# First self attention of a decoder: ScalarE instead of GpSimd makes the high halves of the next pair's weights

## The reference

```python
q, k, v = split_heads(x @ Wq), split_heads(x @ Wk), split_heads(x @ Wv)   # 16 heads of 128
q = _apply_rope(q, cos, sin)
k = _apply_rope(k, cos, sin)
scores = jnp.einsum('bhqd,bhkd->bhqk', q, k) * scale
scores = jnp.where(causal[None, None], NEG_INF, scores)
attn = jax.nn.softmax(scores, axis=-1)
ctx = jnp.einsum('bhqk,bhkd->bhqd', attn, v)
...
x = _layernorm(x + _L0_attn_ref(x, L0_attn_Wq, L0_attn_Wk, L0_attn_Wv, L0_attn_Wo), axis=-1)
```

## Time and profile before

| what | value |
|---|---|
| median of three runs | 2584.72 us (2582.74 to 2585.06) |
| the profiled execution | 2586.08 us, its span 2584.2 us |
| TensorE busy | 2410.7 us, 93% |
| VectorE busy | 1848.7 us, 72% |
| ScalarE busy | 1578.1 us, 61% |
| GpSimd busy | 882.4 us, 34% |
| mean granted clock of TensorE | 0.974 of full speed |

### The profile page before, as it was taken

One profiled execution on the slowest core, in us unless ns is written; L12 is line 12 of the kernel. 1 busy time (PEld: TensorE's weight loads), 2 busy tenths in 40 slices (PEclk: granted clock), 3 DMA queues, 4 the chain that ended last, 5 costly groups with the idle time before them and its releaser, 6 DMA issues. The chain is left out here.

```text
span 2584.2 us, 57959 instructions
## 1 busy us (share of the span) xinstructions
PE 2410.7 (93%) x21584; PEld 1560.9 (60%) x21584; DVE 1848.7 (72%) x3371; ACT 1578.1 (61%) x2718; POOL 882.4 (34%) x800
## 2 busy tenths in 40 slices
PE   7999998989999999999998999999999999999874
PEld 4555555556766677665465666765566666665332
DVE  5777777757777777875665666666678888883597
ACT  5777776258888888884235565652477777772242
POOL 5666666634433444354142122235100011013111
PEclk9999999999999999999998999999999999999987
DMA  3433334426666766676422434353388777787200
GB/s 94 89 75 89 77 88 106 128 46 117 118 123 122 117 115 118 121 128 149 158 91 52 96 86 93 94 112 111 58 146 145 145 146 147 143 150 154 59 1 33
DMA packets 769429, 273.84 MB, mean 106 GB/s; under 512 B 737904, under 2 KB 740720, under 8 KB 767600
## 3 DMA queue, kind: packets, MB, share of 16 engines
q1 hardware_dynamic: 767504, 265.82, 49.8%
q0 software_dynamic: 1760, 5.77, 0.8%
HBM read 84.55 MB, written 6.44 MB: 35 GB/s over the span
## 5 line engine op out<-in xcount | busy, mean ns | idle before, releaser
L909 ACT ACTIVATE phl<-p,ri 128x1024 bf16<-128x1024 f32 (+4 forms) x512 | 437.4, 854 | 382.2 <-DVE ri L1228 355.6
L1238 DVE SCALAR_TENSOR_TENSOR phl<-p,ri,phl 128x1024 bf16<-128x1024 f32 (+4 forms) x512 | 513.6, 1003 | 143.9 <-issue 122.7
L922 ACT ACTIVATE p<-p,nb 128x1024 f32<-128x1024 f32 (+4 forms) x512 | 435.8, 851 | 52.6 <-DVE nb L1221 38.6
L1305 PE MATMUL ps<-wo_lo,v_hi 128*128 128x128 bf16 x2496 | 441.3, 220 | 0.0
L1304 PE MATMUL ps<-wo_hi,v_hi 128*128 128x128 bf16 x2240 | 397.1, 220 | 24.2 <-DMA wo_hi<-phl 15.3
L1306 PE MATMUL ps<-wo_hi,v_lo 128*128 128x128 bf16 x2240 | 396.8, 220 | 1.2 <-issue 1.2
L1304 PE MATMUL ps<-k_hi,q_hi 128*128 128x512 bf16 (+3 forms) x768 | 272.8, 355 | 20.9 <-DVE nb L1219 18.7
L1305 PE MATMUL ps<-k_lo,q_hi 128*128 128x512 bf16 (+3 forms) x768 | 272.1, 354 | 0.0
L1306 PE MATMUL ps<-k_hi,q_lo 128*128 128x512 bf16 (+3 forms) x768 | 272.0, 354 | 0.0
L555 POOL TENSOR_SCALAR wkv_hi<-raw_kv 128x1024 bf16<-128x1024 f32 (+1 forms) x56 | 50.0, 893 | 639.5 <-PE ps L1306 525.5
L1305 PEld LDWEIGHTS ps<-wo_lo,v_hi 128*128 128x128 bf16 x2496 | 245.6, 98 | 33.6 <-issue 0.5
(11 more groups left out here) (206 smaller groups left out, 6130.5 us busy)
## 6 DMA issues: line engine op xcount, KB each, us to landing
raw_kv<-in_wkvself SPq DMA_DIRECT2D x32, 512.0 KB
raw_q<-in_wqself SPq DMA_DIRECT2D x32, 256.0 KB
raw_q<-in_woself SPq DMA_DIRECT2D x32, 256.0 KB
raw_q<-in_wqcross SPq DMA_DIRECT2D x32, 256.0 KB
raw_q<-in_wocross SPq DMA_DIRECT2D x32, 256.0 KB
wo_hi<-phl SPq DMA_TRANSPOSE x384
wo_lo<-phl SPq DMA_TRANSPOSE x384
raw_kv<-in_wkvcross SPq DMA_DIRECT2D x24, 256.0 KB
```

Source lines behind the costliest of these rows:

```text
L909: nc.scalar.activation(m["ph"](qt, w), m["p"][:, qt % 2, 0:w], ACT.Copy, scale=ri[:, qt % 2:qt % 2 + 1]).then_inc(p_norm, 1)
L922: nc.scalar.activation(prob, prob, ACT.Exp, scale=1.0 if L.rms else -1.0, bias=nb[:, qt % 2:qt % 2 + 1], accum_out=rs[:, qt % 2:qt % 2 + 1 ...
L1238: nc.vector.scalar_tensor_tensor(out=m["pl"](qt, w), in0=m["p"][:, qt % 2, 0:w], scalar=ri[:, qt % 2:qt % 2 + 1], in1=m["ph"](qt, w), op0= ...
L1305: nc.tensor.matmul(o, l(0), r(1), start=False, stop=False)
```

## The change

ScalarE gets a new function `weights_high`, called in each slot of self0 behind `job_parts`. In the slots for which `split_plan` has pieces it waits for the weights and the jobs as GpSimd did, copies the high half with a plain rounding copy and raises `w_hi`. GpSimd skips its part 0 in this stage; its part 1 is unchanged and waits on `w_hi`. The splits ahead of the first unit (`start_layer`), those of the output weights and those of the other stages stay on GpSimd.

```diff
@@ GpSimd, unit
                         for kind, part in pieces:
+                            if L.rope and part == 0:
+                                continue
                             if part == 0:
                                 pool.wait_ge(w_in[j], at(lambda n: c[f"win{j}"] + (32 if j == 0 or not L.gqa else 16) * (n // 4 + 2), n, it))
                                 pool.wait_ge(job_mm, at(lambda n: c["job"] + L.before(n), n, it))
@@ ScalarE
+                def weights_high(n, it, qt):
+
+                    j, pieces = L.split_plan(n, qt)
+                    for kind, part in pieces:
+                        if part:
+                            continue
+                        act.wait_ge(w_in[j], at(lambda n: c[f"win{j}"] + 32 * (n // 4 + 2), n, it))
+                        act.wait_ge(job_mm, at(lambda n: c["job"] + L.before(n), n, it))
+                        act.nop(nofuse=True)
+                        cols = 2 * L.chunks * HD
+                        if kind == "kv":
+                            hi, src = wkv[0][:, j, 0:cols], raw_kv[:, j, 0:cols]
+                        else:
+                            hi, src = wq[0][:, j, :, :].rearrange("p c d -> p (c d)"), raw_q[:, j, :]
+                        nc.scalar.activation(hi, src, ACT.Copy).then_inc(w_hi, 1)
+
@@ ScalarE, unit
                         job_parts(n, it, qt, L.jobs(n, qt))
+                        if L.rope:
+                            weights_high(n, it, qt)
                         if qt == QT - 1 and n:
                             heads_out(n - 1, it)
                         if L.rope and qt == 1:
```

## The result

The changed kernel takes 2627.61 us (median of four runs, 2626.49 to 2632.89) against 2584.89 us for the kernel before: a ratio of 1.0157, 95% interval 1.0142 to 1.0173. It is slower by about 41 us by this ratio; the two medians are 42.7 us apart.

The account below looks back on a forecast made before the run. The prediction took the ScalarE-VectorE ring in self0, joined by GpSimd, as the bound. 14 odd units x 3.2 us = 44.8 us more gave 2629.5 us against the 2584.72 median; own range 2625 to 2635, widened to 2614 to 2640.

Parts of the forecast that it names:

- The ring of ScalarE and VectorE: self0: ScalarE and VectorE pass work to and fro in fixed order, setting 12.77 us a unit; GpSimd joins at `q_hi`.
- The moved low half: GpSimd, slot 0: low half waits for ScalarE's high half, delaying the Q multiply; `q_hi` 3.07 to 3.31 us late.
- the next rounding of ScalarE: ScalarE's rounding at 109.42, behind `q_hi` and `q_lo`: 3.0 to 3.2 us late; 3.2 us a unit taken.
- the sum: Total loss over 14 odd units of self0: 14 x 3.2 = 44.8 us, bounds 42 and 49.
- the 0.24 us: Slot 0: VectorE's remainder sits behind the low half, slips in and holds up GpSimd's Q multiply by about 0.24 us.
- The slack at the joint: Where GpSimd's Q add meets ScalarE's `q_hi`: GpSimd late by more than 0.22 us makes the ring late.
- the queries' copy without its cover: ScalarE's Q weights copy, slot 1: free while ScalarE waits before `q_hi`; without that cover 14 x 0.6 = 8.4 us.
- GpSimd waited 8.0 us for the high half, not 5: Sign in the profile after: GpSimd waits for ScalarE's `wkv_hi` some 5 us before the low half.
- The 1.170 us of GpSimd's high half: Price of each of 14 high halves removed from GpSimd, set against 1.057 us for the same work on ScalarE.
- (A): Rival: GpSimd freed means fewer VectorE stretches; 0.5 us in each odd unit, 7 us faster, 2577.6 us; chance 0.03.
- (B): Rival: the 3.2 us come out of ScalarE's gaps before its roundings, so no change, 2585 us; chance 0.04.
- (C): Rival: TensorE, idle 2 us at a time, drops to 1.2 GHz in odd units; 102 us more, 2732 at worst; chance 0.04.

Follow-up runs that it names:

- GpSimd late: Kernel before, with GpSimd starting the split of the keys' and values' weights only after ScalarE's Q copies of the same unit; ratio 1.0180.
- Queries only: Kernel before, with ScalarE making only the high half of the queries' weights; that of the keys' and values' stays on GpSimd; ratio 0.9993.

## Why the prediction was right

**The bound.** The ring of ScalarE and VectorE, with GpSimd joining at `q_hi`, was the right reading: a delay of GpSimd passed through but for about 0.3 us, and nothing came back in the even units (12.84 us). The Q multiply was 3.16 us late in the changed kernel and 3.29 in GpSimd late, and the odd units were 2.86 and 3.05 us longer. The 0.3 us are the 0.27 that GpSimd's K multiply had waited for its ScalarE copy: the K multiply was 2.89 and 3.03 us late, and the units follow it.

**The moved low half.** Forecast 3.07 to 3.31 us of delay at `q_hi`, measured 8.24 - 5.22 = 3.02; the copy took 1.057 us, as its row had said, and the low half 2.13. At the next rounding of ScalarE the forecast was 3.0 to 3.2, and 117.97 - 107.89 = 10.08 against 7.20 gives 2.88. Over 14 odd units 14 x (15.62 - 12.76) = 40.0 us, where the sum had 44.8. That the median of 2627.61 us lies only 1.9 below the forecast of 2629.5 is in part luck: self0 gave less than forecast, and the time behind it, where nothing was forecast, was longer in the profiled execution.

**The term that was too large** is the 0.24 us by which VectorE's remainder was to hold up the Q multiply. The multiply took 1.32 instead of 1.27 us, so it was 0.05. I had taken the 0.24 us from a case with the 512 wide `q_lo`, which ends 0.55 us behind GpSimd's op; the remainder here is 128 wide and ends 0.15 us behind it (113.54 against 113.39). The rest is 0.1 us: GpSimd's ops follow each other without a gap where they don't wait (113.35 is 0.04 before the end of the one ahead).

**The slack was misread.** "The slack at the joint is 0.22 us" holds for `q_hi`, but not for the ring. Queries only shows that `q_hi` can be 0.5 us late at no cost, since GpSimd's K multiply ends `q_lo` in any case. It changed little in the sum, as the K multiply was nearly as late as `q_hi`. But the 8.4 us (0.6 a unit) that I put on the queries' copy without its cover are zero in the order of the kernel before, and about 0.5 us a unit only with the K multiply moved.

**Smaller misses.** GpSimd waited 8.0 us for the high half, not 5; it was idle time and cost nothing more. The 1.170 us of GpSimd's high half is a mean over copies of which some were stretched; the copy of the earlier trace rows took 1.04, no more than ScalarE's 1.057.

**The rivals.** (A) decides where the low half ends before the Q copies; the run with the high half one slot earlier is that case, and it isn't faster (1.0014). There the low half stretched slot 3's remainder, so it shows that the move as a whole won nothing, not what the freed time is worth by itself. (B) was absent. (C), the clock, came in part, and cost nothing in self0, as told below. Behind self0 a lower clock goes with the 9 us that one stretch took longer; whether the change or chance lies behind that isn't shown.

## What to carry to other kernels

Before a step moves from one engine to another, look at what stands in front of it and behind it in both queues. Here 27 us of GpSimd's work went away, ScalarE had room for it (0.10 us a unit when added alone), and the kernel lost 41 us, since the half that stayed behind got a producer 5 us later and kept its place in front of an op on the path. And an op that looks short of slack may be held by another: compare its duration with the same op elsewhere (1.21 against 0.70 us) before counting its idle time.

## What the runs showed of the hardware

TensorE's granted clock in the changed stage is 0.96, over 51 to 408 us, where it was 1.00; columns as in the earlier trace rows.

```profile
51.12:407.70 356.58, 304.31 (x2846) 193.19 (x2844) 243.60 (x550) 246.61 (x527) 177.97 (x126) 0.96 0.33 73
```

It isn't a steady 0.96, but full speed with short stretches at half, 1.2 instead of 2.4 GHz. One of them, TensorE's timeline and three windows:

```profile
61.70 0.22 PE L1324 MATMUL ps<-k_hi,q_hi 128*128 128x128 bf16 x1 [2.13 <-DVE nb L1239]
```

```profile
62.00:63.00 1.00, 1.00 (x7) 0.44 (x5) 0.94 (x3) 0.70 (x3) 1.00 (x2) 1.00 0.00 0
63.00:64.00 1.00, 1.00 (x4) 0.35 (x3) 0.88 (x3) 0.92 (x3) 0.45 (x1) 0.50 0.31 65
...
67.00:68.00 1.00, 1.00 (x6) 0.49 (x5) 0.90 (x2) 0.98 (x4) 0.00 (x0) 1.00 0.00 0
```

TensorE had been idle for 2.13 us, waiting for the maximum that had become late, and after some 1.3 us of full work the clock fell to one half for about 3 us. In the kernel before, the longest idle time of TensorE between 45 and 400 us was 1.3 us, and the clock stayed at 1.00. Of the 14 odd units of the changed kernel, nine have such a stretch. In the odd unit at 107.89 TensorE's longest wait was 1.64 us, and the clock was 1.00 through it; but four more odd units, with waits of 2.16 to 2.19 us, kept 1.00 too. So the length of the wait alone doesn't decide; what does isn't shown. The stretches cost nothing here: the odd units without one take 15.62 or 15.63 us, those with one 15.52 to 15.69.
